# A recommender tower on one core: the turned h is kept in device memory and loaded in rows, instead of being turned on TensorE for every unit

## The reference, cut to what matters

```
h     = q @ w5 + b5                           # 1024 x 300
g     = (v @ v.T)[iu, ju]                     # one number per pair i < j
cross = h[:, iu] * h[:, ju] * g               # 1024 x 44850
f7    = cross @ w7 + b7                       # w7 is 44850 x 300
out8  = concat([h @ w6 + b6, f7]) @ w8 + b8   # 1024 x 300
z     = einsum('bu,bku->bk', out8, labels)    # labels 1024 x 200 x 300
y     = relu(relu(concat([z, dense]) @ top1 + b1) @ top2 + b2) @ top3
```

## Time and profile before

| | busy us | share of the span | instructions |
|---|---|---|---|
| TensorE matmul (PE) | 1686.2 | 92% | 7084 |
| VectorE (DVE) | 1666.4 | 91% | 5850 |
| ScalarE (ACT) | 1028.9 | 56% | 3233 |
| GpSimd (POOL) | 556.3 | 30% | 413 |

### The profile page before, as it was taken

One profiled execution on the slowest core, in us unless ns is written; L12 is line 12 of the kernel. 1 busy time (PEld: TensorE's weight loads), 2 busy tenths in 40 slices (PEclk: granted clock), 3 DMA queues, 4 the chain that ended last, 5 costly groups with the idle time before them and its releaser, 6 DMA issues.

```text
span 1839.3 us, 26080 instructions
## 1 busy us (share of the span) xinstructions
PE 1686.2 (92%) x7084; PEld 1247.3 (68%) x7084; DVE 1666.4 (91%) x5850; ACT 1028.9 (56%) x3233; POOL 556.3 (30%) x413
## 2 busy tenths in 40 slices
PE   2888999999999999999999999999998999997751
PEld 1555667777777777777777777777776777765531
DVE  5999979989999889999999999999999888777776
ACT  3786684674466644465654764456653544464534
POOL 7777508727300226400087028400000000000053
PEclk9889999999999999999999999999999999999975
DMA  9489856848978698989769776997749999989975
GB/s 279 115 282 323 287 167 219 330 158 304 376 301 309 228 358 328 367 329 346 294 206 351 272 257 208 403 419 277 256 155 407 421 407 381 392 320 419 421 302 240
DMA packets 97054, 561.70 MB, mean 305 GB/s; under 512 B 15567, under 2 KB 15941, under 8 KB 71309
## 3 DMA queue, kind: packets, MB, share of 16 engines
q1 hardware_dynamic: 77629, 498.39, 70.5%
q0 software_dynamic: 19264, 61.64, 10.6%
q10 hardware_dynamic: 16, 0.00, 0.0%
HBM read 559.98 MB, written 0.00 MB: 304 GB/s over the span
## 4 chain that ended last, share of the span: by engine, by line
PE 60%; DVE 21%; DMA 8%; POOL 5%; issue 4%; ACT 2%; SPq 0%; DVEq 0%; ACTq 0%; POOLq 0%
PE acc L1010 53%; DVE junk L628 10%; DMA w_sb<-in_w 7%; DVE qa L670 6%; DVE prod L780 5%; POOL x L571 3%; PE coarse L859 2%; POOL lab L571 2%; DMA lab<-in_labels 1%; PE acc L925 1%; PE misc L932 1%; ACT waste L1130 1%; PE acc L891 1%; PE acc L906 1%; PE acc L909 1%
## 5 line engine op out<-in xcount | busy, mean ns | idle before, releaser
L1010 PE MATMUL acc<-w_sb,prod 128*128 128x300 f32 (+2 forms) x5648 | 1522.1, 420 | 50.9 <-DMA w_sb<-in_w 32.7
L1010 PEld LDWEIGHTS acc<-w_sb,prod 128*128 128x128 f32 (+2 forms) x5648 | 1040.6, 191 | 394.8 <-DMA w_sb<-in_w 43.9
L1235 ACT ACTIVATE prod<-prod,g_all 128x256 f32<-128x256 f32 (+4 forms) x1615 | 685.9, 469 | 465.2 <-DVE prod L780 462.8
L571 POOL DMA_INDIRECT x<-in_tbl,ids_sb x368 | 479.2, 1302 | 652.2 <-DVE qa L670 546.2
L780 DVE TENSOR_TENSOR prod<-fine,coarse 128x1280 f32<-128x1280 f32 (+4 forms) x325 | 424.6, 1312 | 97.4 <-PE coarse L859 93.7
L628 DVE SCALAR_TENSOR_TENSOR junk<-lab,heads 128x300 bf16<-128x300 f32 x1208 | 478.1, 464 | 7.2 <-DMA lab<-in_labels 7.1
L628 DVE SCALAR_TENSOR_TENSOR junk<-x,heads 128x300 bf16<-128x300 f32 x1128 | 445.4, 463 | 21.7 <-DMA x<-in_tbl,ids_sb 21.6
L670 DVE SCALAR_TENSOR_TENSOR qa<-x,ex,qa 128x300 f32<-128x300 f32 x612 | 276.1, 532 | 0.0
L602 POOL TENSOR_TENSOR x<-x,out 128x2400 f32<-128x2400 f32 x5 | 26.2, 5254 | 597.2 <-ACT out L1105 588.7
L1130 ACT ACTIVATE waste<-x 128x300 bf16<-128x300 f32 x368 | 161.5, 439 | 24.5 <-DMA x<-in_tbl,ids_sb 24.3
L1054 ACT ACTIVATE picked<-hh 128x256 f32<-128x256 f32 (+4 forms) x325 | 121.5, 374 | 0.0
(11 more groups left out here) (107 smaller groups left out, 520.9 us busy)
## 6 DMA issues: line engine op xcount, KB each, us to landing
w_sb<-in_w SPq DMA_DIRECT2D x320, 750.0 KB, 6.7
lab<-in_labels SPq DMA_DIRECT2D x146, 1200.0 KB, 8.9
x<-in_labels SPq DMA_DIRECT2D x54, 1200.0 KB, 11.2
x<-in_tbl,ids_sb POOLq DMA_INDIRECT x368, 5.7
w_sb<-in_w SPq DMA_DIRECT2D x5, 450.0 KB, 5.9
prod<-in_v_i SPq DMA_DIRECT2D x1, 710.0 KB, 4.3
prod<-in_v_j SPq DMA_DIRECT2D x1, 710.0 KB, 7.4
w_sb<-in_w SPq DMA_DIRECT2D x1, 703.1 KB
```

Of the source, the lines that this page charges most:

```text
L571: pool.indirect_dma_start(out=row_of(t, n), out_offset=None, in_=tables[n], in_offset=bass.IndirectOffsetOnAxis(ap=ids_sb[:, t, n:n + 1], ...
L1010: last = pe.matmul(acc[:, t % 3, 0:EMB], prod[0:rows, u % RING, m, t % 2 * P:(t % 2 + 1) * P], w7_sb[0:rows, u % W7_RING, m * EMB:(m + 1) ...
L1235: act.activation(chunk, chunk, ACT.Copy, scale=g_all[0:rows, pair:pair + 1]).then_inc(chunk_ready, 1)
```

## The change

After TensorE has made h of a tile, a new burst "around" turns it once (four transposes of 112 columns). ScalarE copies the result into `big` and stores it in device memory, in `turned_h[pair, row, tile slot]`, once for each pair of tiles in which the tile takes part, thus twice for all but the first and the last. From there ScalarE's own DMA queue loads the rows that a unit needs: its window six units ahead into a ring of 6 (`window`), and the rows of `fine` where a part begins. In the folded unit that is 4 loads, in the strip units 3, else 1. A row holds the 256 examples of both tiles, 1 KB. VectorE's cross reads `window` in SBUF instead of `coarse` in PSUM. The picks, the repeats, the fills and the transposes of windows are gone, with their copies. qt and h come one unit earlier (LEAD = 9 instead of 8), so that "around" finds its place, and the plan is made with that. The order of chunks in w7 and g within a unit, and of rows in two of the parts, is adapted on the host.

```diff
@@ plan(), schedule()
-            held = bool(rest) and c > STARTS[rest[0][1]] - 8
+            held = bool(rest) and c > STARTS[rest[0][1]] - LEAD
-            at[(STARTS[t] - 7) * FINE + 2] = ("qt", t, 0)
-            at[(STARTS[t] - 6) * FINE + 2] = ("h", t, 0)
+            for n, name in enumerate(("qt", "h", "around")):
+                at[(STARTS[t] - LEAD + 1 + n) * FINE + 2] = (name, t, 0)
+def load_steps():
+    steps = {}
+    for u in range(TOTAL):
+        start = max(at for at in STARTS if at <= u)
+        earliest = start - LEAD + 5
+        if begins_part(u):
+            steps.setdefault(max(u - WINDOWS, earliest), []).append(("fine", u))
+        steps.setdefault(max(u - WINDOWS, earliest), []).append(("window", u))
+    return steps
@@ buffers
-        hh = sb("hh", [P, 4, HH])
+        hh = sb("hh", [P, 3, HH])
-        dup = sb("dup", [P, 2, 2, P])
-        picked = sb("picked", [P, RING, 2, P])
+        window = sb("window", [P, WINDOWS, 2 * P])
+        turned_h = nc.dram_tensor("turned_h", [PAIRS, HH, 2 * P], F32)
@@ cross(u)
-                dve.wait_ge(coarse_ready, u + 1)
+                dve.wait_ge(window_loaded[u % WINDOWS], 16 * windows_to(u))
-                window = coarse[0:rows, u % 2, slot * P:(slot + n) * P]
+                cols = window[0:rows, u % WINDOWS, slot * P:(slot + n) * P]
@@ TensorE
-            def turn_coarse(u):
-            def turn_fine(u, n):
+            def turn_around(t):
+                for c in range(TURNS):
+                    last = pe.transpose(scratch(t)[0:HT, c * P:(c + 1) * P],
+                                        hh[:, t % 3, c * HT:(c + 1) * HT], ident[:])
+                done(last)
-                    if m == 0 and u + 2 < TOTAL:
-                        turn_coarse(u + 2)
@@ ScalarE
-            def pick_window(u):
-            def repeat_fine(u, n):
-            def copy_fine(u, n):
+            def load(what, u):
+                new = first_tile_at(u)
+                if new is not None:
+                    act.wait_ge(h_stored, 16 * stores_before(new + 1))
+                slot, tiles = slots_of(u)
+                cols = slice(slot * P, (slot + tiles) * P)
+                for at, rows, fine_row, fine_step, row, step in strips_of(u):
+                    if what == "fine":
+                        shifts = shifts_of(u)
+                        place = part_count(u) % PLACES
+                        act.dma_start(fine[at:at + rows, place, 0:shifts, cols],
+                                      turned_rows(u, fine_row - shifts + 1, [fine_step, rows], [1, shifts])
+                                      ).then_inc(fine_loaded[place], 16)
+                    else:
+                        act.dma_start(window[at:at + rows, u % WINDOWS, cols],
+                                      turned_rows(u, row, [step, rows])).then_inc(window_loaded[u % WINDOWS], 16)
...
+                elif name == "around":
+                    copy(big[0:HT, 0:TURNS * P], acc[0:HT, of % 3, :])
+                    act.wait_ge(copied, made + 1)
+                    for pair in pairs_of(of):
+                        act.dma_start(turned_h[pair % PAIRS, :, of % 2 * P:(of % 2 + 1) * P].rearrange(
+                            "(c r) b -> r c b", c=TURNS),
+                            big[0:HT, 0:TURNS * P].rearrange("r (c b) -> r c b", c=TURNS)).then_inc(h_stored, 16)
-                    if m == 1 and u + RING < TOTAL:
-                        pick_window(u + RING)
+                    if m == 1:
+                        for what, v in LOAD_STEPS.get(u, ()):
+                            load(what, v)
```

More of the change, by code:

```diff
@@ L46 @@
 HH = 448
+TURNS = 4
+HT = HH // TURNS
+PAIRS = 3
+WINDOWS = 6
+LEAD = 9
 FG = 5
@@ L117, in shifts_of, with first_tile_at, strips_of, windows_to @@
     return FOLDED if phase_of(u)[0] == 2 else FINE
-def fills_of(u):
-    return (shifts_of(u) + 1) // 2
 def begins_part(u):
     return u % UNITS in PART_AT
-def fills_up_to(u):
-    return sum(fills_of(v) for v in range(u + 1) if begins_part(v))
+def first_tile_at(u):
+    return next((t for t in active(u) if STARTS[t] == u), None)
+def strips_of(u):
+    phase, k = phase_of(u)
+    if phase < 2:
+        return [(0, P, EMB * (1 - phase) + P * phase, 1, P * phase + FINE * k + 1, 1)]
+    if phase == 2:
+        base = 2 * P + THIRD
+        return [((2 * half + n) * COARSE, COARSE, base - FOLDED * half + n, 0, base + 1 + n, FINE)
+                for half in range(2) for n in range(LEFT)]
+    return [(n * THIRD, THIRD, 2 * P, 1, 2 * P + 3 * FINE * k + 1 + FINE * n, 1) for n in range(3)]
+def windows_to(u):
+    return sum(len(strips_of(v)) for v in range(u % WINDOWS, u + 1, WINDOWS))
+def fines_to(u):
+    return sum(len(strips_of(v)) for v in range(u + 1)
+               if begins_part(v) and part_count(v) % PLACES == part_count(u) % PLACES)
+def load_steps():
[7 more added lines that the diff above has]
+    return steps
 def slots_of(u):
@@ L136, in slots_of, with pairs_of, pair_at @@
     return slots[0], len(slots)
-def hh_at(t):
-    return t % 2 * 2 + t // 2 % 2
+def pairs_of(t):
+    return [p for p in (t - 1, t) if 0 <= p < TILES - 1]
+def pair_at(u):
+    return min(min(active(u)), TILES - 2)
 def gathers(t):
@@ L483, in dlrm_tower, with turned_rows, stores_before @@
         row8 = heads[:, :, EMB + 1:EMB + 1 + EMB // 2]
-        def hh_cols(u, start, *tail):
-            tiles = active(u)
-            cols = hh[:, bass.ds(hh_at(tiles[0]), 1), bass.ds(start, 1)]
-            step = hh_at(tiles[-1]) - hh_at(tiles[0])
-            return bass.AP(tensor=cols.tensor, offset=cols.offset,
-                           ap=[list(cols.ap[0]), [max(step, 1) * HH, len(tiles)]]
-                           + [list(dim) for dim in tail])
-        HEAD_BURSTS = [("qt", 0, 0), ("h", 0, 0)] + [("fill", 0, n) for n in range(fills_of(0))]
+        def turned_rows(u, row, *dims):
+            slot, tiles = slots_of(u)
+            base = turned_h[pair_at(u) % PAIRS, row:row + 1, slot * P:(slot + tiles) * P]
+            return bass.AP(tensor=base.tensor, offset=base.offset,
+                           ap=[[step * 2 * P, count] for step, count in dims] + [[1, tiles * P]])
+        def stores_before(t):
+            return sum(len(pairs_of(v)) for v in range(t))
+        HEAD_BURSTS = [("qt", 0, 0), ("h", 0, 0), ("around", 0, 0)]
         steps_in_order = HEAD_BURSTS + [BURSTS[tick] for tick in sorted(BURSTS)] + END_BURSTS
@@ L999, in _ @@
                 burst(name, of, n, 0)
-            for u in range(2):
-                turn_coarse(u)
             for u in range(TOTAL):
@@ L1221, in _ @@
                         sum_abs(1, n)
-                if name == "h":
-                    for u in range(RING):
-                        pick_window(u)
+            for step in sorted(LOAD_STEPS):
+                if step < 0:
+                    for what, u in LOAD_STEPS[step]:
+                        load(what, u)
             act.wait_ge(g_ready, 2)
```

128 lines of the change are left out of this document (28 added, 100 removed).

## The result

The changed kernel takes 1926.0 us (median, 1922.2 to 1929.6) against 1842.7 us of the kernel before on the same chip: 4.6% slower, ratio 1.0456 with the interval 1.0439 to 1.0474. The forecast of 1834 us is wrong, and so is its range, whose upper end was 1862 us. The profiled execution spans 1923.9 us, at a mean granted clock of 0.94.

A forecast was written before the change was run, and what follows sets the result against it. TensorE and VectorE were taken to end nearly together from 300 to 1400 us, DMA to bound the end. Terms -19 + 4 - 8 + 9 + 4 = -10 us gave 1834 us from a median of 1843.5; range 1812 to 1862.

The forecast's parts named there:

- Starts of tiles, 4 us forecast: At six starts ScalarE waits for the store before the next chunks' scalings: 0.7 us each, 4 us more.
- ScalarE's queue waits behind SP's: Rival, chance 0.24: stores take turns with w7 rows and hold ScalarE at starts, 5 us each, 30 in all, 1860 us.
- The DMA engines, nothing between 240 and 1392: New loads and stores, a share of 0.077 on some 0.81, fit beside the rest from 240 to 1392 us.
- the stall and the tail: Added DMA traffic at the 1397 us stall costs 4 us; from 1645 to 1757, where DMA sets the end, 9 us.
- VectorE's cross, +20 ns: VectorE's cross, reading the window from SBUF instead of PSUM, takes 20 ns more a unit; ends -3 and +39 ns.
- The rule on SBUF sources: Rival: crosses some 65 ns shorter from SBUF, time 1821 us; given 0.04 of a case with chance 0.16.
- TensorE's part, -19 and -8: Transposes gone from TensorE: 19 us less from 240 to 1392 us, as VectorE's idle time allows; 8 less from 1420 to 1610.
- Head, 0: The first cross waits some 5 us longer for store and load, covered by the gathers' last wait: cost 0, ends 0 and 6.
- The plan, "cancels within 6 us": At the 1397 us stall, last pooled one unit earlier and two more slabs ahead of w7 cancel within 6 us.

The follow-up runs named there:

- e2: Changed kernel with one block a tile in device memory, stored once in 112 rows of 2 KB instead of two stores of 448 rows: 1892.0 us.
- e11: e2 with windows and fine rows loaded only the first time a place is filled (output not the reference's): 1850.5 us.
- e9: e7 with windows and fine rows after the first six units loaded by SP's queue, before w7 loads four units behind: 1909.4 us against 1913.3.
- e6: Kernel before with one more load a unit on ScalarE's queue, rows as a window has, to a place nothing reads: 1856.6 us.
- e10: e2 with the cross reading its coarse operand from PSUM, whatever lies there; loads and stores stay: 1867.2 us.
- e5: Changed kernel with starts planned four units earlier, plus window transposes back on TensorE for nobody: 1920.8 us, 15.9 over the same without them.
- e12: e2 with both edits, no reloads (as e11) and the cross's coarse operand from PSUM (as e10): 1824.8 us, ratio 0.9918 to the kernel before.
- e4: Kernel before with only qt and h one unit earlier (LEAD 9) and the plan made with that: 1847.3 us, ratio 1.0031.
- e7: Changed kernel with one store a tile in 2 KB rows and starts planned four units earlier (LEAD 13): 1913.3 us.

## Why the prediction was wrong

From 1926.0 down to 1824.8 in steps: stores in wide rows 34 us, cross from PSUM 25, no reloads 42. The last 16.5 of these lie below the kernel before; they are the gain that the costs had hidden. The forecast had 4 us for the first, 20 ns a cross for the second, and 13 us for the third.

- **Starts of tiles, 4 us forecast.** This is the step that failed first. It let the store land in the gathers' 5.7 us. It landed in 11.7 us in the median and 28.9 at most, and the units before seven starts lost some 81 us, in which later causes have their part too; the stores alone are worth the 34. The rival "ScalarE's queue waits behind SP's" had the mechanism, turn by turn, and even the condition (a landing above 8.4 us). Its landing of some 17 us was too short for the longest ones: I let a row wait for one w7 packet of SP's queue. At 1035 and 1224 us GpSimd's gathers take turns as well, so a turn is 0.39 us and not 0.26, and at 792 SP's packets are larger than w7's rows (7.2 KB in the mean). And I cut my own 8 us a start to 5 because SP's queue is idle for a fifth of the time; at the longest starts it isn't. That its 30 us come near the measured 34 is partly luck, then. (A gather has 3 packets an engine, 19264 on q0 for 400 gathers, and not the 2 of that argument.)
- **The DMA engines, nothing between 240 and 1392.** The load itself was right: 0.077 of all engines forecast, 8.3% measured on q10. "It fits beside the rest" was wrong. A mean share of 0.81 hides stretches that are full, and w7 has only four units of lead. 500:600 went from 0.82 to 1.00. The trace of before already had a load of w7 in its chain at 1000 us, which the earlier trace rows and the prediction passed over:

```profile
999.96 18.21 DMA w_sb<-in_w
```

Of the 42 us, 13 stood in the sum (4 and 9, for the stall and the tail, where 11 us were measured in the last thirty units). By unit, the traces of e2 and e11 part by 14 us between 250 and 1397 us, where the forecast had nothing, and by 29 behind that, where it had the 13. e9 moved the loads to another queue and won 4 us of 1913; e6 put rows like the windows' beside the kernel before, at 15 us. Both point to traffic, whatever queue issues it.

- **VectorE's cross, +20 ns.** It took 1484 ns, the end of -3 ns. The rule on SBUF sources (page "VectorE: DVE Perf Modes" of the Trainium skill, on the TRN2 errata) would have had it near 1420, an estimate (65 ns less than 1487); the rows deny that a second time. But I asked only what the cross takes and not what it holds: 25 us in the changed kernel, 11.5 in the kernel before, through GpSimd's gathers. No term and no rival had it. The trace of before showed it, in gathers of 4.26 and 0.95 us in turn, one held by a run of L670 and one let through in the cross:

```profile
304.77 4.26 POOL L571 DMA_INDIRECT x<-in_tbl,ids_sb  x1 [0.30 <-issue]
309.34 0.95 POOL L571 DMA_INDIRECT x<-in_tbl,ids_sb  x1 [0.30 <-issue]
```

The Trainium skill, page "SBUF — State Buffer", section "Who interferes with whom", says that a VectorE instruction with two SBUF inputs contends with a GpSimd instruction that reads SBUF; a gather reads its ids there, and the trace agrees with 5.51 us against 4.26 and 0.95, though not every run of such instructions holds a gather (the kernel before at 439.7 us, under e10).

- **TensorE's part, -19 and -8.** Nearly right. e5 gives 15.9 us for the windows' turns alone, and e12, with both causes gone, is 16.5 us faster with LEAD 9 (5.7) still against it: some 22 us together, an estimate, against 27 forecast.
- **Head, 0.** The first cross starts at 104.3 us and not at 98.9, and unit 0 is 5.5 us late. I had the gathers' last wait take that up; it is 5.77 us long now, much as before, only 4.5 us later. Even so the delay is made good by the first tile's units: e12 is 4.3 us late at unit 0 and 2.4 at unit 30, and e4, with LEAD 9 and no new head, is 2.5 late there. The 0 was right, the reason for it wasn't shown.
- **The plan, "cancels within 6 us".** 5.7 us, against the change.

## What to carry to other kernels

Count a small transfer in packets and in turns, against every queue that is busy at that moment, and price it in the stretch where it falls, not at the mean share. Before an operand moves from PSUM to SBUF, look at what GpSimd does in the same units, and whether VectorE's neighbouring instructions read SBUF twice: a regular pattern of long and short instructions in the trace before is the sign. Work taken from a busy engine is worth its full price only if what replaces it touches nothing that was covered, so build the variant with each new cost removed, one at a time and together.

## What the runs showed of the hardware

- Three DMA queues that are busy together are served packet by packet in equal numbers: 806, 768 and 825 packets in 20 us at sizes of 6.5, 3.2 and 0.5 KB. Two stores of 56 rows an engine landed after up to 28.9 us; one store with half the bytes, in 7 rows an engine, after 8.4 at most in e2 and 17.6 in e7.
- GpSimd's gathers take longer when VectorE's tensor_tensor has both operands in SBUF: 1286 to 1332 ns in the mean in the seven kernels with the cross from PSUM, 1623 to 1678 in the nine with it from SBUF, whatever traffic there was. Where a run of scalar_tensor_tensor from SBUF stands before such a cross, a gather was seen to last through both (5.51 us); not every such run holds one.
- A cross of 1280 columns takes the same from PSUM and from SBUF (1487 and 1484 ns).
